# A decoder on one core: the first stage's input goes to two buffers per lane and is fetched by SyncE one item ahead

## The reference

```
x = _layernorm(x + _L0_attn_ref(x, ...))
x = _layernorm(x + _L0_xattn_ref(x, ctx_768, mask, ...))
...
def _L0_attn_ref(x, ...):
    x = x + min_gru(rmsnorm(x, w_rms_mix), Wg, bg, Wv, bv, Wd, bd)
    x = x + sliding_attn(rmsnorm(x, w_rms_attn), Wqkv, Wo)
    x = x + glu_ffn(rmsnorm(x, w_rms_ffn), Wgate, Wup, Wout)
    return x
```

## Time and profile before

| | |
|---|---|
| median of 3 runs | 2599.33 us (2593.41 to 2608.83) |
| the profiled execution | 2605.69 us, of which its span is 2603.5 us |
| PE busy over the span | 2288.2 us, 88% |
| ACT busy over the span | 1484.2 us, 57% |
| DVE busy over the span | 1451.9 us, 56% |
| POOL busy over the span | 299.4 us, 11% |
| mean granted clock of TensorE | 0.971 |
| inputs issued by ACT (line 911) | 30 transfers of 64 KB, 1.8 us from issue to landing |

### The profile page before, as it was taken

The page is one execution under the profiler, slowest core; times in us unless marked ns, Lnnn a source line. Parts: engine busy times, 40 slices in busy tenths (PEclk is TensorE's granted clock), DMA queues, the critical chain, the costliest instruction groups (busy, mean ns, idle before and its releaser), DMA issues.

```text
span 2603.5 us, 99769 instructions
## 1 busy us (share of the span) xinstructions
PE 2288.2 (88%) x44994; PEld 1764.3 (68%) x44994; DVE 1451.9 (56%) x3437; ACT 1484.2 (57%) x3532; POOL 299.4 (11%) x404
## 2 busy tenths in 40 slices
PE   2988989889887489999999999989999999999997
PEld 2777777777775266776767767667667677676775
DVE  2555555555554555565565655665656556655564
ACT  1456556555564155565665665656656656565564
POOL 1011011011110011000100111001001110011000
PEclk8999999999999599999999999999999999999998
DMA  4000000000000100000000000000000000000000
GB/s 121 8 10 9 11 11 10 10 10 10 10 10 16 45 6 7 7 6 9 7 7 9 6 6 8 6 8 7 7 9 6 7 7 7 9 7 7 7 6 4
DMA packets 56068, 30.74 MB, mean 12 GB/s; under 512 B 24673, under 2 KB 53794, under 8 KB 55650
## 3 DMA queue, kind: packets, MB, share of 16 engines
q1 hardware_dynamic: 51330, 22.45, 3.2%
q10 hardware_dynamic: 4320, 1.97, 0.3%
HBM read 19.15 MB, written 5.24 MB: 9 GB/s over the span
## 4 chain that ended last, share of the span: by engine, by line
PE 41%; DVE 13%; ACT 11%; issue 2%; DMA 0%; SPq 0%; DVEq 0%
PE bank L1268 5%; PE bank L1335 2%; PE bank L1465 2%; PE bank L1298 2%; PE bank L378 2%; ACT PT L1520 2%; PE bank L1398 2%; ACT zels L1520 2%; DVE zels L553 2%; PE bank L1458 1%; DVE h L1781 1%; PE bank L1384 1%; DVE m L551 1%; PE bank L1308 1%; PE bank L1367 1%
## 5 line engine op out<-in xcount | busy, mean ns | idle before, releaser
L1178 POOL TENSOR_TENSOR PT<-zels,unit 128x512 f32<-128x512 f32 x160 | 206.9, 1293 | 1468.4 <-ACT zels L1520 1281.6
L1520 ACT ACTIVATE zels<-bank 128x512 f32<-128x512 f32 (+1 forms) x256 | 142.5, 573 | 154.6 <-PE bank L1384 78.4
L1520 ACT ACTIVATE PT<-bank 128x512 f32<-128x512 f32 x256 | 147.9, 598 | 92.9 <-PE bank L1441 49.8
L471 DVE TENSOR_REDUCE top_of<-bank 128x4 f32<-128x512 f32 x256 | 160.4, 684 | 26.3 <-PE bank L403 19.7
L1384 PE MATMUL bank<-zels 64*64 64x64 f32 x5120 | 154.9, 220 | 3.5 <-issue 3.5
L378 PE MATMUL bank<-w_gate,ident 128*128 128x128 f32 (+3 forms) x448 | 146.9, 411 | 0.0
L1382 PE MATMUL bank<-zels 64*64 64x64 f32 x4096 | 136.2, 223 | 11.5 <-DVE zels L1748 6.7
L1520 ACT ACTIVATE W<-bank 128x512 f32<-128x512 f32 x192 | 114.0, 594 | 53.4 <-PE bank L1398 27.9
L1382 PEld LDWEIGHTS bank<-zels 64*64 64x64 f32 x4096 | 114.0, 134 | 37.2 <-issue 29.5
L1384 PEld LDWEIGHTS bank<-zels 64*64 64x64 f32 x5120 | 132.8, 135 | 8.4 <-issue 4.4
L568 ACT ACTIVATE rstd<-bank,eps 128x128 f32<-128x128 f32 x224 | 82.1, 366 | 68.8 <-PE bank L1193 46.4
(11 more groups left out here) (322 smaller groups left out, 5741.2 us busy)
## 6 DMA issues: line engine op xcount, KB each, us to landing
ctxT<-in_ctxT_dram SPq DMA_DIRECT2D x64, 48.0 KB, 1.8
x_after_cross_attention<-x SPq DMA_DIRECT2D x32, 64.0 KB, 1.5
h<-x_after_cross_attention SPq DMA_DIRECT2D x8, 256.0 KB, 2.8
xin<-x_after_cross_attention SPq DMA_DIRECT2D x32, 64.0 KB, 1.9
out_dram<-xn SPq DMA_DIRECT2D x32, 64.0 KB, 1.6
x<-in_xT_dram ACTq DMA_DIRECT2D x30, 64.0 KB, 1.8
input_integers<-xq SPq DMA_DIRECT2D x8, 128.0 KB, 2.0
xq<-input_integers SPq DMA_DIRECT2D x32, 32.0 KB, 1.8
```

Of the source, the lines that this page charges most:

```text
L471: dve.tensor_reduce(top, b[u][:, :].rearrange("p (a j k) -> p a j k", a=2, j=2), AX_X, ALU.max)\
L1178: pool.tensor_tensor(n.TI[:, k % 2, :, :], (n.PT0, n.PT1)[k % 2][:, :, 1, :], unit[:, :].unsqueeze(1).broadcast_to([P, NP, DK]), ALU.add)\
L1520: ins = act.activation(out, src, func, **how)
```

## The change

`x0` gets two buffers per lane, and item `it` uses buffer `it % 2`; the four readers take that one. The transfer leaves ACT's stage `load`, which is then empty, and goes to SP's loop as `load_x`. SP calls `load_x(s, it + 1)` between the context of item `it` and the store of item `it - 1`. It waits for `sq1` of item `it`, so that at most one transfer of a lane is counted at a time, and for `xr` of item `it - 1`, the last reader of the buffer that is written.

```diff
-            n.x0 = buf("x0", [P, P])
+            n.x0 = buf("x0", [P, 2, P])
...
+                def load_x(s, it):
+                    if it > 0:
+                        sp.wait_ge(pg.pool[s], pg.PO.upto(it - 1, "sq1"))
+                    if it > 1:
+                        sp.wait_ge(pool_did[s], PO.upto(it - 2, "xr"))
+                    if it > 0:
+                        sp.sem_inc(waits_passed, 1)
+                    sp.dma_start(lane[s].x0[:, it % 2, :], a["xT"][it * LANES + s]).then_inc(pg.loaded[s], 16)
...
                 for s in range(LANES):
-                    sp.dma_start(lane[s].x0[:, :], a["xT"][s]).then_inc(pg.loaded[s], 16)
+                    load_x(s, 0)
                 for it in range(ROUNDS):
                     for s in range(LANES):
                         load_context(s, it)
+                        if it + 1 < ROUNDS:
+                            load_x(s, it + 1)
                         if it > 0:
                             store(s, it - 1)
...
-                        front(pool.tensor_tensor(n.sqf[:, :], n.x0[:, :], n.x0[:, :], ALU.mult), "sq1")
+                        front(pool.tensor_tensor(n.sqf[:, :], n.x0[:, it % 2, :], n.x0[:, it % 2, :], ALU.mult), "sq1")
...
-                        pool.tensor_tensor(n.x3[:, :], n.x2[:, :], n.x0[:, :], ALU.add).then_inc(pool_did[s], PO.step(s, "xr"))
+                        pool.tensor_tensor(n.x3[:, :], n.x2[:, :], n.x0[:, it % 2, :], ALU.add).then_inc(pool_did[s], PO.step(s, "xr"))
...
-                    elif stage == "load":
-                        if it > 0:
-                            act.wait_ge(pool_did[s], PO.upto(it - 1, "xr"))
-                            act.dma_start(n.x0[:, :], a["xT"][it * LANES + s]).then_inc(pg.loaded[s], 16)
```

More of the change, by code:

```diff
@@ L796, in advance @@
                         pool.wait_ge(pg.dve[s], pg.DV.upto(it, "scan"))
-                        front(pool.tensor_tensor(n.xf[:, :], n.hf[:, 3 * P:4 * P], n.x0[:, :], ALU.add), "x1")
+                        front(pool.tensor_tensor(n.xf[:, :], n.hf[:, 3 * P:4 * P], n.x0[:, it % 2, :], ALU.add), "x1")
                         front_did("x1")
@@ L975, in advance @@
                         dve.wait_ge(pg.act[s], pg.AC.upto(it, "rms1"))
-                        front(dve.scalar_tensor_tensor(n.xnf[:, :], n.x0[:, :], w_rms[:, 0:1], n.rstdf[:, :], ALU.mult, ALU.mult), "xn1")
+                        front(dve.scalar_tensor_tensor(n.xnf[:, :], n.x0[:, it % 2, :], w_rms[:, 0:1], n.rstdf[:, :], ALU.mult, ALU.mult), "xn1")
                     elif stage == "gdv":
```

## The result

| | before | after |
|---|---|---|
| median, runs on the same chip | 2596.47 us (2593.41 to 2608.83) | 2566.64 us (2565.35 to 2567.47) |
| profiled execution, its span | 2605.69 us, 2603.5 us | 2567.47 us, 2565.4 us |
| first stage, span | 784 us | 746.65 us |
| rest of the program, span | 1771.5 us | 1770.75 us |
| mean granted clock | 0.971 | 0.972 |

The changed kernel takes 0.9876 of the time before, with a 95% interval of 0.984 to 0.991. The forecast was 2568 us, in a range of 2558 to 2582.

A forecast was written before the change was run, and what follows sets the result against it. PE was taken to set the first stage's pace, waiting 30.5 us for POOL's square; 1.45 + 0.70 us a round, scaled to 31 us over 15 rounds with no added costs, took 2599.3 to 2568 us, range 2558 to 2582.

The forecast's parts named there:

- The wait goes entirely: PE's first-stage wait at L814 for POOL's square of the input: from 30.5 us in 30 waits to under 2.
- Lane 0, 1.45 us: Lane 0's change of items: ACT's L568 starts about 1.45 us sooner, and this reaches PE's next wait whole.
- Lane 1, 0.70 us: Lane 1's change of items: PE gains 0.70 us, with ACT's L568 held until L444 ends.
- Sum of a round: Both lanes: 2.15 us in the round followed, scaled by 30.5/32.0 to 31 us in 15 rounds; bounds 28.5 to 33.5.
- SP at no cost: Fifteen more input issues per lane on SP, about 0.33 us each, cost nothing; bounds 0 to 1 us once.
- POOL at no cost: POOL's square runs 5 us earlier beside other DVE work, counted at no cost.
- The bound of 12 us: Upper bound of POOL's cost: each of 30 squares holds DVE for its whole 0.40 us.
- The remaining waits "neither grow nor vanish": PE's other first-stage waits come from PE's own work a step before, so they shift with it, unchanged in size.
- Absorbed: Rival: the next limit, ACT's chain or DVE beside the square, stands closer; gain 16 us, 2583 us; chance 0.11.
- The better clock: Rival: the first stage's four clock falls, blamed on idle time behind lane 1's L814, vanish; 2562 us; chance 0.11.
- The worse clock: Rival: the shorter round brings a clock fall in each of 15 rounds, 11 more, 18 us; chance 0.03.
- That the change does nothing: Rival: SP issues the input so late that PE's wait for the square stays; 2599 us; chance 0.05.

The follow-up runs named there:

- The kernel with `sums` first: Changed kernel with lane 1's softmax sums (L461, L463) ahead of lane 0's last gate exponential (L959) in ACT's list; 2589.04 us, 0.9959 of before.

## Why the prediction was right

**The wait goes entirely: right.** L825 has no entry in the steady part, where under 2 us were allowed. The square starts right behind the add in both lanes and is ready 4.1 us early in lane 0 and 3.6 in lane 1 (455.73 - 452.09). From the recorded rows 4.3 and 3.7 come out.

**Lane 0, 1.45 us: right, with an excess of 0.1.** From L858 to L847 PE took 6.04 us; the same pair, L869 to L858, now takes 4.48: 1.56 us less. ACT's L568 stands 0.54 us behind L953's start in place of 2.01, 1.47 sooner, by its 1.39 us of idle time and the overlap of two rows. That it starts as soon as L953 lets it is what the step said.

**Lane 1, 0.70 us: too small.** PE took 4.62 us from L882 to L867 and takes 3.75 now, 0.87 us less. I had held L568 back to the end of L444's row, which allowed 0.76 us for ACT. But the two start 0.28 us apart though L444's row takes 0.39, in all 15 rounds.

**Sum of a round: the term that was mis-sized.** In the pair of changes that the rows follow, 2.15 us were worked out and 1.56 + 0.87 = 2.43 measured. Scaling from this pair to the mean was right: I had taken 30.5/32.0, or 0.953, and 2.32/2.43 is 0.955. The 15 rounds so gave 34.7 us where I had 31, more than the upper bound of 33.5. That bound allowed 0.1 us a place for rows that overlap once the wait is gone. PE's L825 now starts 0.17 us before the end of L869's row in lane 0 and 0.16 before the end of L893's in lane 1, which is about 5 us in 30 places in place of 3. The stage shrank to 746.65 us where 755 were forecast, by this, by the clock in the first item and by 3 us at its two edges.

**The time, 2568 us: met by mechanism and some luck.** The term was 3.7 us too small, and the fifth fall, which I had not counted on, takes 1.6 back. Medians of four runs scatter on top: the gain between them was 29.8 us here and 33.8 us when the changed kernel was run again. That 2566.64 lies 1.4 us from the forecast is closer than the sum deserves.

**SP at no cost: right.** The kernel without transfers is 0.5 us from the changed one, within its scatter.

**POOL at no cost: right for its rows.** The square's row, 32 times in the changed kernel, first to last start:

```profile
L800 POOL TENSOR_TENSOR ls<-x x32: 398/401/403, 48.9 to 727.0; 128x128 f32<-128x128 f32 x32
```

The median of 401 ns stands against 398 before. 3 ns in 30 squares are 0.1 us. The Trainium skill (GPSIMD Engine Reference, section 1, Specifications) allows contention with DVE instructions that have two SBUF inputs or use the two-port mode. The trace shows 3 ns here, but it is no test of the first case: beside the square DVE works on L476 in lane 0 and L987 in lane 1, and each reads a PSUM bank. The bound of 12 us was far too wide.

**The remaining waits "neither grow nor vanish": not quite.** L893 kept its 8.0 us, but `AO`'s wait grew by 1.9 us, the one for `Qa` is new with 3.8, that for `h` shrank by 3.5 and that at L411 by 1.0. They sum to +1.2 us in 15 rounds, which the 2.32 us a round already contain. With the 30.5 us that went this leaves 29.3, and the trace has 29.7 us less idle time.

**The rivals.** Absorbed: the limit did stand close, as L858's wait shows, but took only tenths. The better clock was wrong in direction: with less idle time there are five falls, not four, and they stand at another place of the round, so "each time behind the stretch of lane 1" held for the kernel before alone. The worse clock has the counts on its side, as a matter of the round's length, and the wrong size: one more fall where it asked for eleven. The kernel with `sums` first, at 45.96 us and 10 falls, is nearest to it. That the change does nothing is excluded; only the kernel with two buffers that doesn't fetch ahead does nothing.

The rise of the clock in the first item was foreseen by no step. It adds 3.2 us to the gain of the profiled execution, 38.1 us; most of the rest above 29.8 is a profiled execution of the kernel before that lay 9.2 us above its median.

## What to carry to other kernels

When a transfer is late, look first at what the issuing engine has in front of it, and at when its old buffer was free: here 3.7 us lay between the two, and an issue on an idle engine gained as much with one buffer as with two. Follow the wait two steps on, to what is late next, before you price it; and where engines run fixed lists, read on the next engine what an order changed on one will meet there. Compare rounds that the clock left alone, take their mean and not the shortest, and count the falls apart. Before you fill idle time against a fall of the clock, look where in the round the falls of this very kernel stand.

## What the runs showed of the hardware

- A transfer issued by ACT has a row of 0.34 us and delayed the next activation by 0.28 us (0.46 against 0.18 from L440 to L458); of that the round felt 0.11 us.
- Two activations that don't depend on each other (L444 and L568) start 0.28 us apart though the first has a row of 0.39 us.
- A fall of TensorE's clock from 2.4 to 1.2 GHz makes a round of this stage up to 1.6 us longer (46.62 against 45.02). The falls come at two places of the round, 17 and 41 us behind lane 0's mean, with PE busy for 2.7 or for 3.6 of the 4 us ahead; the same 2.7 come in every round, mostly without a fall. Their number was 5 in six profiles at 44.99 to 45.02 us a round, 7 at 45.13 and 45.30, 10 at 45.96. A change of 0.1 us a round may so cost or give several microseconds more than it should.
- In the first item the clock rose at 64 us in five of the profiles and at 74 us in the other seven. The five all fetch early; the seven are the three that fetch late and four that fetch early. Its cause stays open.
- The transfer took 2.6 us from issue to landing on SP's queue behind the context and mask, and 1.8 us alone, on ACT's queue or on SP's (one buffer). With 24 us to spare neither matters.
